# GpSimd's output step split in two, and the heads' normalisation made to wait for the squared scales

## What is computed

```python
x = x + layernorm(attn(layernorm(x)))      # 16 heads, latent k and v of 64, scores times a decay, softmax
x = x + layernorm(ffn(layernorm(x)))       # ffn: Hadamard, 4-bit activations, ternary weights

scale = clip(max(abs(x @ H), axis=-1), 1e-05) / 7          # per token
xq = clip(round(x @ H / scale), -8, 7) * scale
ffn = einsum('bsi,oi->bso', xq, ternary(weight))
```

## Time and profile before

| | us |
|---|---|
| median of 3 runs | 1443.37 |
| lowest, highest | 1438.68, 1443.58 |
| the profiled execution | 1434.7 |
| its span, first to last instruction | 1432.6 |

### The profile page before, as it was taken

One profiled execution on the slowest core, in us unless ns is written; L12 is line 12 of the kernel. 1 busy time (PEld: TensorE's weight loads), 2 busy tenths in 40 slices (PEclk: granted clock), 3 DMA queues, 4 the chain that ended last, 5 costly groups with the idle time before them and its releaser, 6 DMA issues.

```text
span 1432.6 us, 37419 instructions
## 1 busy us (share of the span) xinstructions
PE 1277.3 (89%) x12850; PEld 566.9 (40%) x12850; DVE 1229.8 (86%) x2744; ACT 1137.9 (79%) x1225; POOL 926.8 (65%) x1438
## 2 busy tenths in 40 slices
PE   5889999999999999999999999999999999999852
PEld 3333444444334344434444443444344343444331
DVE  7658999998999898998998999989989989898654
ACT  1788888887888887888888888888878888888921
POOL 5135766766676667676666776756676766666557
PEclk9799999999999999999999999999999999999975
DMA  5464565655655564664556466555646645556320
GB/s 181 147 189 150 164 196 182 201 175 163 208 165 166 165 201 141 201 196 141 180 184 196 154 195 208 159 164 172 199 139 207 193 139 183 183 159 196 106 62 31
DMA packets 174560, 241.39 MB, mean 168 GB/s; under 512 B 28464, under 2 KB 145200, under 8 KB 174512
## 3 DMA queue, kind: packets, MB, share of 16 engines
q1 hardware_dynamic: 140176, 206.68, 45.4%
q10 hardware_dynamic: 34336, 34.08, 7.5%
HBM read 154.70 MB, written 69.21 MB: 156 GB/s over the span
## 4 chain that ended last, share of the span: by engine, by line
PE 48%; DVE 27%; issue 12%; ACT 7%; POOL 2%; SPq 1%; DMA 1%; DVEq 0%; ACTq 0%; POOLq 0%
PE heads_ps L762 17%; PE scores_ps L749 10%; DVE diagonal L1349 9%; PE misc_ps L678 7%; ACT probs L967 4%; PE misc_ps L634 4%; DVE weighted L1257 3%; DVE ln_stats L1190 3%; DVE v_sb L1234 3%; PE misc_ps L605 2%; DVE xscale L1313 2%; DVE heads L1246 2%; DVE absmax L1307 2%; PE misc_ps L720 1%; PE misc_ps L711 1%
## 5 line engine op out<-in xcount | busy, mean ns | idle before, releaser
L967 ACT ACTIVATE probs<-scores_ps 128x1024 f32<-128x1024 f32 x768 | 765.8, 1024 | 181.6 <-PE scores_ps L749 180.8
L762 PE MATMUL heads_ps<-probs,v_sb 128*32 128x512 f32 x4096 | 525.5, 608 | 4.3 <-DVE heads L1246 2.4
L1349 DVE TENSOR_TENSOR diagonal<-scores_ps,comp 128x1024 f32<-128x1024 f32 x256 | 312.3, 1220 | 109.6 <-PE scores_ps L749 109.3
L749 PE MATMUL scores_ps<-q_rep,k_rep 64*128 64x128 f16 (+2 forms) x5120 | 327.2, 252 | 63.0 <-DVE diagonal L1349 51.0
L749 PEld LDWEIGHTS scores_ps<-q_rep,k_rep 64*128 64x128 f16 x5120 | 162.5, 95 | 355.9 <-DVE diagonal L1349 150.1
L974 ACT ACTIVATE probs<-diagonal 128x2048 f32<-128x2048 f32 x128 | 245.5, 1918 | 0.0
L1065 POOL TENSOR_TENSOR ln_neg_mean<-zero,ln_moments 128x4 f32<-128x4 f32 (+1 forms) x98 | 19.9, 203 | 242.5 <-DVE ln_moments L1198 242.4
L762 PEld LDWEIGHTS heads_ps<-probs,v_sb 128*32 128x32 f32 x4096 | 95.5, 109 | 171.5 <-issue 169.6
L1111 POOL TENSOR_TENSOR q_hl<-weighted,q_hl 128x768 f16<-128x768 f32 x64 | 105.9, 1654 | 64.9 <-DVE q_hl L1264 64.9
L1257 DVE SCALAR_TENSOR_TENSOR weighted<-misc_ps,edges 128x384 f32<-128x384 f32 x256 | 127.8, 541 | 7.0 <-PE misc_ps L634 5.4
L678 PE MATMUL misc_ps<-wo,heads_c 128*128 128x256 f32 x504 | 124.8, 391 | 0.0
(11 more groups left out here) (155 smaller groups left out, 1708.5 us busy)
## 6 DMA issues: line engine op xcount, KB each, us to landing
q_rep<-q_scratch SPq DMA_DIRECT2D x128, 384.0 KB, 4.0
k_rep<-k_scratch SPq DMA_DIRECT2D x256, 192.0 KB, 4.5
q_scratch<-q_hl SPq DMA_DIRECT2D x64, 384.0 KB, 2.4
k_scratch<-k_hl SPq DMA_DIRECT2D x64, 384.0 KB, 3.4
x_in<-in_L_attn_x_dram ACTq DMA_DIRECT2D x32, 512.0 KB, 4.3
heads_c<-heads SPq DMA_DIRECT2D x256, 64.0 KB, 3.3
den_spread<-den_scratch SPq DMA_DIRECT2D x256, 64.0 KB, 2.3
x_res<-in_L_attn_x_dram ACTq DMA_DIRECT2D x32, 512.0 KB, 6.1
```

Of the source, the lines that this page charges most:

```text
L749: ins = mm(scores_ps[:, place + par, at:at + n * P], k_rep[rows, pair, kv_, k_cols], q_rep[rows, pair, qv_, q_cols], start=True, stop=True)
L762: ins = mm(heads_ps[W32 * g:W32 * (g + 1), :], v_sb[:, b.slot, kt, at:at + W32], probs[:, quad % 2, g, kt, :], start=(kt == 0), stop=(kt = ...
L967: nc.scalar.activation(flat[:, :, at:at + S], scores_ps[:, place:place + 2, :], ACT.Exp, scale=EXP_SCALE).then_inc(off_probs, 1)
L1349: v.tensor_tensor(diagonal[:, quad % 2, 2 * two:2 * two + 2, :], scores_ps[:, place:place + 2, :], comp[:].rearrange("p t n -> p (t n)").u ...
```

## The change

`add_out` becomes `norm_out` (the four normalisations) and `add_x1` (the addition). In the pipeline `norm_out` stays where `add_out` was; `add_x1` goes behind the low half of k's second part, ahead of `x_apply`, and waits for `qint_ready` of batch "b" of the same iteration. `heads_normalize` waits, in every iteration that has a "b", for `square_ready` of that batch. The opening iterations without "c" have neither step; the closing list uses `add_out`, which calls both, without the new waits.

```diff
 POOL_STEPS = [
-    ("x1_apply", "b"), ("q", 0, "pre"), ("rstd4", "c"), ("k", 0, "pre"), ("add_out", "c"), ("heads_normalize", "a"), ("k", 1, "pre"),
+    ("x1_apply", "b"), ("q", 0, "pre"), ("rstd4", "c"), ("k", 0, "pre"), ("norm_out", "c"), ("heads_normalize", "a"), ("k", 1, "pre"),
+    ("add_x1", "c"),
     ("x_apply", "load"), ("q", 1, "pre"), ("rstd2", "a"),
 ]
...
-            def heads_normalize(b):
+            def heads_normalize(b, scaled=None):
+                if scaled is not None:
+                    pool.wait_ge(square_ready, scaled.done)
                 pool.wait_ge(heads_compacted, count(128, b, 128))
                 pool.wait_ge(den_spread_done, count(128, b, 128))
...
-            def add_out(b):
+            def norm_out(b):
                 m = ln[4]
                 pool.wait_ge(ln_ready[4], b.done)
...
                 ins.then_inc(ffn_normed, 1)
+
+            def add_x1(b, rounded=None):
                 pool.wait_ge(ffn_normed, b.done)
+                if rounded is not None:
+                    pool.wait_ge(qint_ready, rounded.done)
                 nc.gpsimd.tensor_tensor(out_sb[:, b.rows], out_sb[:, b.rows], x1[:, b.slot, b.rows], ALU.add).then_inc(out_ready, 1)
...
+            def add_out(b):
+                norm_out(b)
+                add_x1(b)
...
-                        steps[name](b.other(DISTANCE_OF[group]), *part)
+                        if name == "heads_normalize" and present["b"]:
+                            heads_normalize(b.other(DISTANCE_OF[group]), b.other(DISTANCE_OF["b"]))
+                        elif name == "add_x1":
+                            add_x1(b.other(DISTANCE_OF[group]), b.other(DISTANCE_OF["b"]))
+                        else:
+                            steps[name](b.other(DISTANCE_OF[group]), *part)
```

More of the change, by code:

```diff
@@ L1127, in add_out @@
                 ins.then_inc(ffn_normed, 1)
+            def add_x1(b, rounded=None):
                 pool.wait_ge(ffn_normed, b.done)
+                if rounded is not None:
+                    pool.wait_ge(qint_ready, rounded.done)
                 nc.gpsimd.tensor_tensor(out_sb[:, b.rows], out_sb[:, b.rows], x1[:, b.slot, b.rows], ALU.add).then_inc(out_ready, 1)
-            steps = {"rstd2": lambda b: rstd(2, b), "rstd4": lambda b: rstd(4, b), "heads_normalize": heads_normalize, "add_out": add_out,
+            def add_out(b):
+                norm_out(b)
+                add_x1(b)
+            steps = {"norm_out": norm_out, "add_x1": add_x1, "rstd2": lambda b: rstd(2, b), "rstd4": lambda b: rstd(4, b), "heads_normalize": heads_normalize, "add_out": add_out,
                      "q": lambda b, c: split(b, "q", c), "k": lambda b, c: split(b, "k", c), "x_apply": x_apply, "x1_apply": x1_apply}
```

## The result

| | before | after |
|---|---|---|
| median, us (4 runs each) | 1442.19 | 1369.88 |
| lowest, highest | 1438.68, 1443.58 | 1367.58, 1374.99 |
| the profiled execution | 1434.7 | 1374.99 |
| its span | 1432.6 | 1373.0 |

The changed kernel takes 0.9507 of the time before, with a 95% interval of 0.9474 to 0.9539. The forecast was 1381 us, in a range from 1366 to 1403.

What follows compares the result with a forecast made beforehand. GpSimd's heads_c held VectorE's xscale_sq; TensorE waited about 2 us and the clock sometimes fell. Gains of 49.0 + 6.5 = 55.5 us from 1434.7 gave 1379, plus 2 of surplus 1381, range 1366 to 1403.

Steps and rivals of the forecast that it cites:

- Step (1): heads_c on GpSimd waits for the squares: xscale_sq's hold and the clock falls go, 49.0 us gained, no cost on GpSimd.
- the five of 40.08: Five earlier iterations where heads_c started late and xscale_sq took 0.13 us, taken as a sample of the change's order.
- Step (2): The addition leaves its old place beside xscale: the reciprocal comes up to 0.73 us earlier; 6.5 us gain taken.
- The upper bound of 19.7 us: Most that removing the addition from beside xscale could gain: 0.73 us in all 27 iterations, if all reaches the end.
- Step (3): The addition behind k's second split and the quantize fits GpSimd's idle time: zero cost, 11 us if VectorE's cover is gone.
- the rule of the Trainium skill: Casts and GpSimd operations contend, the second waits for the whole other: beside the cast, at worst the whole 2.37 us lost.
- The surplus: The 8.7 us by which the runs' median before exceeded the profiled execution; 2 us of it added to the forecast.
- The clock did not go on falling: Rival: another TensorE pause still brings the clock fall, 16.6 us come back, 1402 us; chance 0.07.
- The hold did not move: Rival: the hold only moves to the quantize and the cast on VectorE, no change, 1438 us; chance 0.08.
- The loop through the squares: Rival: heads_c, now behind the previous batch's FFN, makes y late if squares are late; slower, 1456 us; chance 0.07.

Runs made afterwards that it cites:

- The reduction: The kernel before with one line changed: the square made by a tensor_reduce with multiply over a repeated view instead of a product; 1386.22 us, 0.9637.
- the wait alone: The changed kernel with the addition of x1 back in its old place, the wait of heads_normalize for the squares kept; 1385.95 us, 0.9622.
- the five extra reductions: The changed kernel with five reductions into an unread tile behind xscale_sq on VectorE, which then stands for 3.05 us; 1465.47 us, 1.021.
- the move: The changed kernel without the wait of heads_normalize for the squares, only the addition of x1 moved; 1375.69 us, 0.9542.
- The further comparisons: The unaltered changed kernel timed twice more against the kernel before, beside later experiments; 1371.5 us (0.954) and 1373.07 us (0.9558).

## Why the prediction was right, and where its sizes were off

**The view of what bounds the kernel** was right: the held square, TensorE's wait behind it and the fall of the clock behind that. The reduction took away the hold alone and gained what the wait alone gains; the five extra reductions put the wait back alone and brought back the falls.

**Step (1)**, 49.0 us, measured 45.75 with the wait alone. The difference is the 0.12 us by which 27 iterations of 40.20 are longer than the five of 40.08 that stood as the sample: in 19 of the 27 `xscale` is held for longer than in any of the five. As a cost of the wait on GpSimd I had zero, and `heads_c` is in time: it ends 2.75 us before y starts in the iteration shown, and 1.77 at the least. What the step didn't see is that the move gives the same gain without the wait, as far as these runs can tell. I had priced the move by the earlier reciprocal only, and not asked when GpSimd would come to `heads_c` once the addition was gone from ahead of it. For the sum of both parts that made no difference; for the parts alone, 6.5 us for the move was far off the 64 measured.

**Step (2)** is the term of the sum that was mis-sized: 6.5 us taken, 17.0 measured (27 times 40.08 - 39.45 = 0.63). I took 0.24 us from one TensorE group of the earlier trace rows. Two neighbours of it in the same timeline of the kernel before were as long, and I did not count them:

```profile
261.01 0.72 PE L749 MATMUL scores_ps<-q_rep,k_rep 64*128 64x256 f16 x8
...
266.79 0.85 PE L749 MATMUL scores_ps<-q_rep,k_rep 64*128 64x256 f16 x8
```

In the iteration shown above the three take 0.61, 0.62 and 0.61. So the waits inside them were 0.11, 0.24 and 0.24, in sum 0.59, nearly the 0.63 per iteration. Group by group, TensorE's lead over the kernel before is nothing ahead of the first of the three, 0.58 us behind the last, and stays 0.58 to the end of the iteration. The upper bound of 19.7 us was the better guide. The two experiments agree: the changed kernel's 39.45 is 0.75 us below the 40.20 with the wait alone, close to the 0.73 by which `xscale` is shorter.

**Step (3)** took zero, and no loss shows. The quantize is still held, by 0.25 us (0.94 against 0.69). The cast, which I let meet the addition's last 0.4 us, did not meet it in the iteration shown: the addition ran from 26.8 to 29.2 us of the iteration, where the prediction had it from 27.7 to 30.1, and the cast began at 29.5 (29.7 before). In two early iterations it met it and was held for 0.2 and 0.3 us. With k's weighting moved ahead the cast lasts 0.58 to 1.41 us in all 27, and the iterations are still 39.45. So the rule of the Trainium skill that spoke against this place (page "SBUF — State Buffer", section "Who interferes with whom") agrees with these rows for the cast too, but here the hold cost nothing.

**Not foreseen** were the long iteration from 238.64 (43.31 - 39.45 = 3.9 us) and the opening, 2.6 us longer. In both TensorE waits some 3 us for k's weighting and the clock falls; the prediction asked for 1.00 in all 27 windows, and 26 have it. So the profiled execution came out at 1375.0, where the sum said 1379: 10.5 us more from (2), less the 6.5 of these two, with 0.2 from the closing. That the two numbers are so near is in part luck, since these errors run against each other.

**The surplus.** I had added 2 of the 8.7 us by which the median of before lay above its profiled execution. In the first comparison the other runs of the changed kernel lie 5 to 7 us below its profiled execution, so this was the other 7 us of the miss. The further comparisons gave differences of 64.8 and 62.7 us, the first one 72.3; the profiles differ by 59.7. So 8 to 10 us of the first difference did not come back, and no reading of a trace would have given them.

**The rivals.** The clock did not go on falling, but for the one long iteration. The hold did not move: square 0.13, quantize 0.94, cast 0.56 us in the iteration shown. The loop through the squares has more cover than before, 2.75 us against 2.2, since the square comes earlier.

**Still open.** Why the DMA that the reciprocal awaits is late in that one iteration was not tried. SP issues it 11.5 us into the iteration there and 10.3 us in an ordinary one; what held SP up is not shown.

## What to carry to other kernels

A tiny operation whose median is ten times its minimum may be waiting for something that has no row of its own: look at what runs on GpSimd until it ends. Before ordering two engines by a wait, see whether the operation can be written in a form that is not held; here one line, a reduction in place of a product, gained as much as the wait. One operand in SBUF is no guarantee: `xscale`, the quantize and the cast have one, and were held. And when a stage's releaser comes earlier, add up the waits inside all the TensorE groups behind it, not that of one.

## What the runs showed of the hardware

Where an operation of VectorE already waited for a GpSimd instruction and GpSimd had its next one ready, VectorE went first: the quantize kept its 0.94 us and the addition was held instead (2.82 against 2.38). The reciprocal of 128x4 numbers between the two held operations of the kernel before was never held (178 ns in the median and at the most), and the product written as a reduction took 0.13 us under `heads_c`. The cast of 128x768 numbers, 0.56 us alone, lasted up to 1.41 us beside GpSimd's addition.

The granted clock fell to 0.50 in 13 of 27 iterations behind a wait of TensorE of 2.2 us, in 8 of 22 behind one of 2.0 to 2.1, and in none of 27 behind one of 1.0. Each of these falls lasted about 3.4 us and cost 1.6 to 1.7. That is no fixed price: behind the waits of 2.8 us in the kernel with x1's low half moved, the falls lasted 3.4 or 6.8 us, and an iteration with one was 0.7 or 2.0 us longer than one without.
